# A second tile of every 64 fetched row by row, by ScalarE, in three of six gather passes of a graph network

## The reference

```python
edge_index = jnp.stack([src, dst])
h = relu(layernorm(x));  x = x + (1 + eps) * h + segment_sum(h[src] * edge_weight[:, None], dst)      # L0
h = relu(layernorm(x));  x = x + L1(h)      # h = relu(h @ W + b), then 3 times:
                                            #   agg = segment_sum(w[:, None] * (h @ conv[i])[src], dst); h = gru(agg, h)
                                            #   with w = sum(edge_attr_64_n2 * edge_attr_64, axis=1)
h = relu(layernorm(x));  x = x + L2(h)      # one of 16 relations per edge, attention, sum over dst
h = relu(layernorm(x));  x = x + L3(h)      # mean over the edges of a node (by src), then a matmul
```

## Time and profile before

| | us |
|---|---|
| median of 3 runs | 6547.37 (6542.28 to 6547.39) |
| the profiled execution's own time | 6555.57 |
| its span, first to last instruction | 6553.8 |
| GpSimd busy | 4766.0 (73% of the span) |
| VectorE busy | 3827.2 (58%) |
| TensorE busy, matmuls | 3315.8 (51%) |
| ScalarE busy | 858.8 (13%) |

### The profile page before, as it was taken

How to read it: one execution, slowest core, us unless ns; L and a number is a source line. 1 busy time by engine, 2 the same in 40 slices (tenths; PEclk the granted TensorE clock), 3 DMA queues, 4 the chain that set the end, 5 groups by cost and what they waited for, 6 DMA issues and landing times.

```text
span 6553.8 us, 107755 instructions
## 1 busy us (share of the span) xinstructions
PE 3315.8 (51%) x13560; PEld 2693.6 (41%) x13560; DVE 3827.2 (58%) x13371; ACT 858.8 (13%) x2167; POOL 4766.0 (73%) x5006
## 2 busy tenths in 40 slices
PE   3444445444447555555755554696444444444444
PEld 3333334333334444444444543343333333333333
DVE  6767666666666656656666664454454444444445
ACT  1000001000002111111211110143333333000000
POOL 6777776777774677777677777675777776777775
PEclk9555556555557666666876665696555555555556
DMA  5434442333332222222122222154222222222222
GB/s 140 111 107 110 110 110 74 74 75 75 75 75 53 53 54 54 54 54 53 46 54 53 53 54 54 48 212 140 54 53 54 53 54 55 54 54 54 54 54 59
DMA packets 276003, 471.96 MB, mean 72 GB/s; under 512 B 99701, under 2 KB 181882, under 8 KB 269035
## 3 DMA queue, kind: packets, MB, share of 16 engines
q0 software_dynamic: 156176, 306.05, 19.1%
q1 hardware_dynamic: 84091, 85.05, 3.8%
q10 hardware_dynamic: 35040, 73.87, 3.6%
HBM read 389.33 MB, written 77.27 MB: 71 GB/s over the span
## 4 chain that ended last, share of the span: by engine, by line
POOL 41%; issue 20%; DMA 13%; SPq 12%; PE 11%; DVE 3%; ACT 1%; DVEq 0%; POOLq 0%; ACTq 0%
POOL G L665 40%; DMA G<-h_rows,ix_src 11%; PE ps L769 10%; SPq L540 9%; SPq L532 3%; DMA G<-h_rows 1%; PE ps L826 1%; DMA t_rows<-G 0%; DVEq L1223 0%; DMA G<-t_rows,pos 0%; DVE HNA L1234 0%; SPq L551 0%; DVE bst L1151 0%; DVE M L1214 0%; ACT HG L1703 0%
## 5 line engine op out<-in xcount | busy, mean ns | idle before, releaser
L665 POOL DMA_INDIRECT G<-h_rows,ix_src x3860 | 3703.3, 959 | 1296.5 <-issue 1051.2
L769 PE MATMUL ps<-G,M 128*128 x10000 | 2554.6, 421 | 3081.0 <-SPq L551 2182.9
L769 PEld LDWEIGHTS ps<-G,M 128*128 128x128 f32 x10000 | 2168.9, 310 | 3431.6 <-issue 3425.9
L1234 DVE TENSOR_TENSOR HNA<-HNA,ps 128x128 f32 (+1 forms) x3328 | 957.8, 288 | 1359.8 <-PE ps L769 1338.8
L1214 DVE TENSOR_SCALAR M<-irow,rel,w_l 128x128 f32<-128x128 f32 x3328 | 1207.1, 365 | 180.7 <-issue 174.2
L665 POOL DMA_INDIRECT G<-t_rows,pos x770 | 740.9, 962 | 260.0 <-issue 228.8
L1234 DVE TENSOR_TENSOR HTA<-HTA,ps 128x129 f32 x840 | 243.3, 290 | 518.1 <-PE ps L769 509.7
L1803 ACT ACTIVATE sorting<-sorting,pk 128x128 f32<-128x128 f32 x784 | 250.6, 390 | 1446.9 <-DVE sorting L1409 1444.2
L769 PE MATMUL ps<-sorting 128*128 128x128 f32 x1568 | 435.1, 374 | 0.5 <-ACT sorting L1803 0.3
L1881 ACT ACTIVATE G<-G,pk 128x128 f32<-128x128 f32 x782 | 311.7, 402 | 679.1 <-DMA G<-t_rows,pos 678.7
L1234 DVE TENSOR_TENSOR X<-X,ps 128x128 f32 x832 | 239.1, 287 | 230.0 <-PE ps L769 223.6
(11 more groups left out here) (270 smaller groups left out, 2150.7 us busy)
## 6 DMA issues: line engine op xcount, KB each, us to landing
G<-h_rows SPq DMA_DIRECT2D x7680, 0.5 KB
G<-h_rows,ix_src POOLq DMA_INDIRECT x3860, 2.6
t_rows<-G SPq DMA_DIRECT2D x49, 1024.0 KB, 4.0
HTA<-in_edge_attr_n ACTq DMA_DIRECT2D x50, 500.0 KB
HTA<-in_edge_attr ACTq DMA_DIRECT2D x50, 500.0 KB
G<-t_rows SPq DMA_DIRECT2D x1536, 0.5 KB
sorting<-q_flat ACTq DMA_DIRECT2D x98, 196.0 KB
G<-t_rows,pos POOLq DMA_INDIRECT x770, 2.5
```

The lines of the kernel that those rows point to most:

```text
L665: return nc.gpsimd.indirect_dma_start(to, None, table, bass.IndirectOffsetOnAxis(ap=ix, axis=0))
L769: return nc.tensor.matmul(dst, lhsT, rhs, start=start, stop=stop, skip_group_check=True)
L1234: V.tensor_tensor(to, to, ps[:, u % SLOTS, 0:n], ALU.add).then_inc(s_add, 1)
```

## The change

In L0, in the first pass of L1 and in L3 (`ACT_PASSES`), tile 31 of every 64 (`BY_ACT`) is no longer gathered by POOL. ScalarE fetches its 128 rows by plain DMAs of one row, from a list `act_by_one`, into slot 31 and a new slot 65 in turn. SP waits for these rows in its walk as for its own. ScalarE issues them: in L0 all 128 of the first tile ahead of the zeroing copy L1760, and then half a tile in each turn of its loop, which is now unrolled; in L1 all 128 of the first tile after the second `Qb` load, and then 16 rows after each further `Qb` load; in L3 all tiles one after the other. In all three the first two tiles have a free slot, and the later ones wait for one. The other three passes are gathered as before, except that tile 31 of every odd 64 lies in slot 65 there too.

With it go: two more operations in `steps_of`; a list of edge types, `rel_by_one`, that is now loaded behind the last pass of L1 instead of at the start, in the place of another buffer; four more small list loads and two more list operations in L2; and some small tiles that now share memory.

```diff
+BY_ACT = RING // 2 - 1
+ACT_PASSES = (PASS_L0, PASS_L1, PASS_L3)
+def slot_of(t):
+    if t % (2 * RING) == RING + BY_ROW:
+        return RING
+    return RING + 1 if t % (2 * RING) == RING + BY_ACT else t % RING
...
+        def fetched_by_pool(k, t):
+            return t % RING != BY_ROW and not (t % RING == BY_ACT and k in ACT_PASSES)
...
             def arrivals(k, tiles, fetched, table, listed):
+                    elif t % RING == BY_ACT and k in ACT_PASSES:
+                        j = t // RING
+                        sp.wait_ge(s_rowa[k][j % 2], 16 * P * (c * (ROW_PARTS // 2) + j // 2 + 1))
...
             arrivals(PASS_L1 + LAYERS - 1, ET, EF, h_rows, one_by_one)
             sp.sem_inc(s_list1, 1)
+            sp.wait_ge(s_cix, NB)
+            list_rows(rel_by_one, "edge_type_16", BY_ROW, s_rel)
...
-                    if t % RING != BY_ROW:
-                        gather(G[:, t % RING, 0:D], table, ix[:, t:t + 1]).then_inc(s_g[t % RD], 16)
+                    if fetched_by_pool(k, t):
+                        gather(G[:, slot_of(t), 0:D], table, ix[:, t:t + 1]).then_inc(s_g[t % RD], 16)
...
             def steps_of(key, tb, nb, steps, k0, k1, to_b, to_bb, tau, beside=None):
-                link(V.tensor_single_scalar(odd, odd, RING + BY_ROW, ALU.is_equal))
                 link(V.tensor_single_scalar(to_b[at, :], to_b[at, :], RING - 1, ALU.bitwise_and))
-                link(V.tensor_tensor(to_b[at, :], to_b[at, :], odd, ALU.add))
+                for last, by in ((BY_ROW, 1), (BY_ACT, RING + 1 - BY_ACT)):
+                    link(V.scalar_tensor_tensor(to_b[at, :], odd, float(RING + last), to_b[at, :], ALU.is_equal, ALU.add))
+                    if by > 1:
+                        link(V.tensor_scalar(odd, odd, float(RING + last), float(by - 1), ALU.is_equal, ALU.mult))
+                        link(V.tensor_tensor(to_b[at, :], to_b[at, :], odd, ALU.add))
...
+            def rows_of_tile(k, m, part, parts):
+                c, j = divmod(m, ROW_PARTS)
+                if part == 0 and m >= 2:
+                    act.wait_ge(s_mm, k * S + (m - 2) * RING + BY_ACT + BLK)
+                n = P // parts
+                for e in range(part * n, (part + 1) * n):
+                    if (e - part * n) % RD == 0:
+                        regs = min(RD, n)
+                        _, row = nc.values_load_multi_w_load_instructions(
+                            act_by_one[32 * j:32 * j + 1, c * P + e:c * P + e + regs],
+                            engines=[mybir.EngineType.Activation], min_val=0, max_val=NP - 1,
+                            skip_runtime_bounds_check_because="it lies in its table as every index of a gather does")
+                    act.dma_start(G[e:e + 1, BY_ACT if m % 2 == 0 else RING + 1, 0:D],
+                                  h_rows[bass.ds(row[(e - part * n) % RD], 1), :]).then_inc(s_rowa[k][m % 2], 16)
+            ROW_TILES = ROW_SETS * ROW_PARTS
             act.wait_ge(s_list, 1)
             act.wait_ge(s_hst, 16 * stores(N0))
             for q in range(2):
                 ew_load(q, q)
+            act.wait_ge(s_ones, 16 * 2 * ROW_PARTS)
+            rows_of_tile(PASS_L0, 0, 0, 1)
             act.wait_ge(s_init, NG)
...
-            with act.Fori(0, EW_CHUNKS // 2 - 1) as i:
+            for i in range(EW_CHUNKS // 2 - 1):
+                if 1 + i // 2 < ROW_TILES:
+                    rows_of_tile(PASS_L0, 1 + i // 2, i % 2, 2)
                 for q in range(2):
                     act.wait_ge(s_ewc, 2 * i + q + 1)
                     ew_load(2 * i + 2 + q, q)
...
                         act.dma_start(Qb[:, j % 2, :], q_of[j:j + 1, :].broadcast_to((P, PB * BLK))) \
                             .then_inc(s_qld[j % 2], 16)
+                        if j == 1:
+                            for q in range(2):
+                                act.wait_ge(s_hs[q], two_stores(q, N0))
+                            rows_of_tile(PASS_L1, 0, 0, 1)
+                        elif j >= 2 and 1 + (j - 2) // 8 < ROW_TILES:
+                            rows_of_tile(PASS_L1, 1 + (j - 2) // 8, (j - 2) % 8, 8)
...
             unrolled([(0, n2_out), (2, normalise(N2, into_hn))])
+            act.wait_ge(s_ix, 3)
+            act.wait_ge(s_hst, 16 * stores(N3))
+            for m in range(ROW_TILES):
+                rows_of_tile(PASS_L3, m, 0, 1)
             unrolled([(0, copy_in(N3))])
```

More of the change, by code:

```diff
@@ L177, in gnn_kernel @@
         big = sb("big", [P, R * D])
-        G = sb("G", [P, RING + 1, W1])
+        G = sb("G", [P, RING + 2, W1])
         M = sb("M", [P, MR, P])
@@ L231, in gnn_kernel @@
         c_pre = sb("c_pre", [BLK, NB])
-        starts = sb("starts", [P, NB, HB])
+        chunk_rows = sb("chunk_rows", [P, 2 * NB * HB])
+        starts, jump = [chunk_rows[:, k * NB * HB:(k + 1) * NB * HB].rearrange("p (b h) -> p b h", b=NB)
+                        for k in range(2)]
+        rel_by_one = chunk_rows[:, 0:ROW_SETS * P].bitcast(I32)
         shift = gate[:, 6 * BANK:6 * BANK + NB * HB].rearrange("p (b h) -> p b h", b=NB)
-        jump = sb("jump", [P, NB, HB])
         first3 = sb("first3", [P, BLK])
@@ L363, in gnn_kernel @@
         s_row = [[sem(f"s_row{k}_{q}") for q in range(2)] for k in range(3 + LAYERS)]
+        s_rowa = {k: [sem(f"s_rowa{k}_{q}") for q in range(2)] for k in ACT_PASSES}
         s_ones = sem("s_ones")
         s_ones3 = sem("s_ones3")
+        s_rel = sem("s_rel")
         s_list1 = sem("s_list1")
@@ L433, in of, with uses @@
             return t[:, 0:tiles(g) * P]
-        def uses(u):
-            return len([t for t in range(u, EF, RD) if t % RING != BY_ROW])
+        def fetched_by_pool(k, t):
+            return t % RING != BY_ROW and not (t % RING == BY_ACT and k in ACT_PASSES)
+        def uses(k, u):
+            return sum(fetched_by_pool(j, t) for j in range(k) for t in range(u, EF, RD))
         def nth_use(t):
@@ L504, in _, with list_rows @@
                     .then_inc(s_rows, 16)
-            for to, name in ((one_by_one, "src"), (rel_by_one, "edge_type_16")):
+            def list_rows(to, name, place, done):
                 tile = a[name][0:ROW_SETS * ROW_SET * P].rearrange("(c j t e) -> j c t e", c=ROW_SETS, j=ROW_PARTS, e=P)
                 for j in range(ROW_PARTS):
-                    sp.dma_start(to[32 * j:32 * j + 1, :].rearrange("p (c e) -> p c e", e=P), tile[j:j + 1, :, BY_ROW, :]) \
-                        .then_inc(s_ones, 16)
+                    sp.dma_start(to[32 * j:32 * j + 1, :].rearrange("p (c e) -> p c e", e=P), tile[j:j + 1, :, place, :]) \
+                        .then_inc(done, 16)
+            list_rows(act_by_one, "src", BY_ACT, s_ones)
+            list_rows(one_by_one, "src", BY_ROW, s_ones)
             def h_store(phase, src, ready, at):
@@ L614, in _ @@
             sp.wait_ge(s_list1, 2)
-            for j in range(ROW_PARTS):
-                sp.dma_start(rel_by_one[32 * j:32 * j + 1, :].bitcast(F32).rearrange("p (x e) -> p x e", e=P),
-                             by_tile[j:j + 1, :, BY_ROW, :]).then_inc(s_ones3, 16)
+            for to, place in ((rel_by_one, BY_ROW), (act_by_one, BY_ACT)):
+                for j in range(ROW_PARTS):
+                    sp.dma_start(to[32 * j:32 * j + 1, :].bitcast(F32).rearrange("p (x e) -> p x e", e=P),
+                                 by_tile[j:j + 1, :, place, :]).then_inc(s_ones3, 16)
             for q in range(2):
@@ L774, in one_round @@
                     lists[ROW_SLOT:ROW_SLOT + 1, bass.ds(r * RD, steps)], engines=[mybir.EngineType.PE],
-                    min_val=0, max_val=RING,
-                    skip_runtime_bounds_check_because="a slot is a tile's number modulo RING, or RING itself")
+                    min_val=0, max_val=RING + 1,
+                    skip_runtime_bounds_check_because="a slot is slot_of a tile")
                 _, upto = nc.values_load_multi_w_load_instructions(
@@ L1875, in attend @@
                     slot = u
+                    if u == BY_ACT and half:
+                        slot = RING + 1
                     if u == BY_ROW:
```

25 lines of the change are left out of this document (13 added, 12 removed).

## The result

The changed kernel takes 6641.05 us (median of 4 runs, 6632.73 to 6643.25) against 6544.91 (6542.28 to 6547.39): 1.0147 times as long, 95% interval 1.0133 to 1.016. The forecast was 6563, in a range of 6530 to 6605. The sign was right; the size, 96 us where 16 was forecast, was not, and the time lies outside the range.

What follows compares the result with a forecast made beforehand. POOL's gathers were taken to set the pace throughout. Gathers left out -45.4, stalls +59.0 and `steps_of` +2.1 gave +15.7 us: 6571.3 for the profiled execution, 6563 as median, range 6530 to 6605.

Steps and rivals of the forecast that it cites:

- The later tiles: ScalarE's tiles from 95 on, in L0, L1 and L3: they come in time, so they cost 0.
- three ways to be wrong: 128 ACT rows under 57 or over 65 us; a later ACT tile late in L1; POOL's holes shorter through faster SP catch-up.
- steady 1.25 us from gather 80 on: Sign expected in the profile after: behind each pass's starting stall, POOL's gathers follow one another every 1.25 us.
- Rival C: ScalarE's and SP's rows hinder each other (shared lock or longer landings): 0.50 us a row, 6609 to 6629 us; chance 0.12.
- Gathers left out: POOL gathers 12 tiles fewer in each of L0, L1's first pass and L3, saving 45.4 us in sum.
- ScalarE's tile of rows: 128 one-row DMAs issued by ScalarE take 61.5 us, between 60 and 68, plus 1.3 for landing.
- The stalls: POOL waits for late tile 31 at each pass's start: 15.3 us in L0, 35.2 in L1, 8.5 in L3, sum 59.0.
- The hole of 10 us or more: Sign expected on POOL about gathers 60 to 80 of each of the three passes, 35 us in L1.
- `steps_of`: Longer list operations at the start, ahead of POOL's first gather: 2.1 us more, in full.
- Later tiles in L1 and L3: Tile 95 and later arrive about when POOL needs them: 0; in L1 6 us if a part took 9.2.
- L2, the lists, the zeroing copy: Added L2 list operations, new and moved list loads and moved copy L1760: 0, covered by other work.
- Shared generator: The skill's descriptor-generator lock between ACT's and SP's DMA issues: some 8 us more by it, not counted in the sum.

Runs made afterwards that it cites:

- e1: The changed kernel with ScalarE fetching rows in L1 and L3 only, none in L0: 6555.52 us, 1.0022 of the kernel before.
- e4: e1, but GpSimd gathers tile 31 in L1 and L3 and ScalarE begins with tile 95: 6514.98 us, 0.9958 of the kernel before.
- e12: e1, but in L1 the rows of tile 31 are issued ahead of the wait for VectorE's count and the `Qb` loads: 6532.64 us, 0.9986 of before.
- e9: e4, plus every second of ScalarE's tiles in L0 (95, 223, ...), 32 rows ahead of each pair of loads: 6519.05 us, 0.9965 of before.
- e2: The changed kernel, but in L0 each turn issues 32 rows, two loads, 32 rows, two loads: 6575.58 us, 1.0047 of before.
- e3: e1, with the four edge loads of each L0 turn issued together, without rows: 6555.79 us, 1.0021 of before.

## Why the prediction was wrong

The step that failed is the one under "The later tiles", for L0: "The `ew_load`s now stand behind 64 rows; a turn of ACT is 32 us and 32 steps are 30 gathers, 38 us, so they stay ahead after the first", which was given no price. It took rows and loads in one queue to be independent but for their issue times. The profile shows 41.1 us for the turn, 9.0 of them rows held behind four loads; that is over GpSimd's 37.2 and makes ScalarE the bound of L0. Measured in place of 0: 77 us in the trace, and 81 by e1 against its own kernel before, gone without the rows of L0 and three quarters gone with another order. Only some 5 us lay between the turn and its allowance, and neither a rival nor the sensitivity asked what a turn a sixth longer would cost. None of the three ways to be wrong that it named at its end looks at this turn; of what was to be seen, "steady 1.25 us from gather 80 on" is what failed in L0. The first of these turns came out as forecast ("bring tile 95 to about 194"): its last row was issued by 191.6, and nothing was held in it. Rival C came nearest ("longer landings behind the loads of 500 KB in L0"), but placed the harm at the first tile, where it hardly occurred: in L0 the first tile's first row came behind four loads and its issue took 1.3 us only. The direction was not luck: the forecast stalls alone make e1 slower, by 14.9. But most of the 96 us comes from a place that was priced at nothing.

Point by point, the rest:

- Gathers left out: 12 in each pass, at 1.25 to 1.27. Right.
- ScalarE's tile of rows, 61.5 us forecast. In L0 the rows start at 67.33 and the last is issued by 127.17, with a register load ahead of them 62.3; in L1 60.1; in L3 some 59.5. Right in L0, 1 to 2 too high elsewhere.
- The stalls: 15.8, 35.0, 7.1 measured against 15.3, 35.2, 8.5; sum 57.9 against 59.0. e4 took away the last two for 40.5 us where 43.7 less two gathers were counted. e12 shows the cause of most of L1's. The hole of 10 us or more that was to be seen in each pass is 14.8 us in L0, but 6.1 in L3.
- "It is not given back, as POOL has no slack": right; e1, with two of the three stalls, is 0.2% slower than before.
- `steps_of`: 2.1 forecast, the first gather is 2.3 later, in the twelve experiments, which all kept it, 1.2 to 2.4.
- Later tiles in L1 and L3: forecast 0, and right: behind gather 80 GpSimd has no hole over 1.5 us there. L2, the lists, the zeroing copy: forecast 0. Together with differences from run to run the stretch from L1's last gather of the first pass to L3's first (2153.2 to 5628.5) is 3.0 us shorter than before. Right.
- Shared generator: SP's rows took 0.225 in L3 while ScalarE issued beside it, as in the earlier trace rows, and ScalarE's 0.224. Nothing of a lock shows. The Trainium skill's rule (Perfetto Trace Analysis, section "DMA Instruction — HWDGE (DVE, Sync)") would have asked for a longer issue on one of them; by this trace its 8 us are not there.

With the measured stalls and start the forecast's own sum reads -45.4 + 57.9 + 2.3 = 14.8. For e1, which has no rows in L0, it reads -30.3 + 42.1 + 1.9 = 13.7, and +14.9 was measured. So the mechanism at the starts was read rightly; what was left out is that in L0 the rows share ScalarE's queue with large loads.

## What to carry to other kernels

Before work is put on an "idle" queue, write down the period of that queue with everything in it, beside the period that it must keep. Here 32 us were counted and 37.2 allowed, and 41.1 came of it, because small transfers were held behind large ones. With so little between the two, ask what a longer period would cost. What helped here was to put fewer large transfers ahead of the small ones (three quarters of the loss), to let the queue run empty in between (e9, no hold, though no gain over e4), and to leave the pass with the large loads alone (all of it); another queue was not tried. And don't hand a slower path the first item of a pipeline that starts empty: leaving one tile in 12 to the fast path turned a loss of 0.2% into a gain of 0.4%.

## What the runs showed of the hardware

- A transfer of one row on ScalarE's queue issues in 0.235 us (median) in L0, 0.39 us after the one ahead of it. In the changed kernel it was held for 6.0 to 9.4 us behind four transfers of 500 KB in 20 of 20 turns from 185 us on; behind the first four of L0 it took 1.3 us, and behind the second four, issued when nearly all rows before them had moved, 0.48.
- 1 MB as four transfers of 250 KB held the first row in 38 of 40 cases; as two of 500 KB, the 15th to 18th in 28 of 40 where the queue was kept full (e2) and none in 20 of 20 where it had emptied (e9).
- One transfer of 500 KB alone, with 32 rows ahead of and behind it, held nothing (20 of 20); with 16 rows between such transfers, 49 of 81 times a row was held.
- A pair of loads landed within 13.3 us with four loads together and no rows (e3), and in 19.4 us in a turn of the changed kernel with rows on the same queue.
- Rows issued behind four loads on one queue did not move until the last of the loads' 500 packets had moved (20 of 20 turns, 32 to 35 rows each time).
